# In each table's lookup VectorE waits once until its own second comparison has signalled

## The chip, the core and the metric

The kernel runs on one core of a Trainium2 chip. The metric is the device time of one execution in microseconds, lower is better. A core has TensorE (matmuls and transposes), VectorE, ScalarE, GpSimd and SyncE, each with its own in-order queue of instructions; they order their work among each other by semaphores. 16 DMA engines move data between HBM and the on-chip memories.

## The reference

512 samples each have 26 ids, one into each of 26 embedding tables of 128 columns, and a dense vector of 128. The dot products of all pairs among the 27 vectors are the features of a small network:

```python
e = jnp.stack([tbl_0[ids[:, 0]], ..., tbl_25[ids[:, 25]]], axis=1)
sd = jnp.einsum('bfd,bd->bf', e, dense)
ss = jnp.einsum('bfd,bgd->bfg', e, e)
z = jnp.concatenate([dense, sd, ss[:, iu, ju]], axis=1)
h = jnp.concatenate([z, dense], axis=1)
h = jnp.maximum(h @ W_top1 + b_top1, 0.0)
h = jnp.maximum(h @ W_top2 + b_top2, 0.0)
y = h @ W_top3
```

Everything is float32.

## The kernel before

Fourteen of the tables are read row by row with indirect DMAs by GpSimd (L269), 128 rows each time, and TensorE transposes what arrives (L507). The other twelve, the small ones of 1000 or 1250 rows, are read by matmul: the whole table is loaded into `table` (L221), 125 rows of the partition dimension by 8 or 10 chunks, and multiplied by a one-hot matrix of the ids. This work on one table is called a lookup here, and the tables are counted 0 to 11 in their order; table 3 has ten chunks, the others eight.

A lookup of table t has these steps:

- ScalarE copies the ids, relative to the table's rows, from PSUM to `ids_h` (`relate_ids`, L315).
- ScalarE rounds the table to a shorter float format: `high` (`split_high`, L325), one instruction for the table (two for table 0).
- VectorE makes `onehot`, one comparison for each chunk c (`make_onehot`, L378), 512 samples wide; each signals `onehot_ready`.
- VectorE subtracts `high` from `table` to get the remainder `low` (`split_low`, L386), in two halves of the chunks; each signals `low_ready`.
- TensorE multiplies `high` and `low` of each chunk with `onehot`, sixteen matmuls in one PSUM bank for a table of eight chunks (L472), and signals `table_selected`.
- ScalarE copies the bank into `embT` (L336), which signals `table_placed`.

The buffers `table`, `high`, `low` and `onehot` are threefold, so that the loading of table t + 3 waits for `low` of table t, and VectorE's work on table t + 3 waits for `table_selected` of table t.

VectorE's order is written out by hand in `step` (L390). While TensorE is at table t, VectorE has in its queue for table t + 1: comparisons 0 and 1, the first half of `low`, comparisons 2, 3 and 4 (2 to 5 with ten chunks), the second half of `low`, and the rest of the comparisons. Table 0 stands ahead of that loop (L426) with an order of its own. So the loop makes tables 1 to 11.

TensorE's order is the list `STEPS` (L185): T is a lookup, B a batch of transposes, D the dots of 128 samples (L527), C the copies of the dots into `pairs` (L309 on ScalarE, L371 on VectorE), L, M and Y the three layers. For the last two tables, 10 and 11, the lookup before D0 takes only the first 256 samples, and the other 256 come after D0 (L485). D0, the first dots, waits for all of `embT`'s first 128 samples (L511 to L517), thus also for ScalarE's copy of table 11's result. GpSimd's gathers are paced by `table_selected` (L264), and some later ones by `dots_done` (L266). After its last comparison VectorE adds two weight blocks (L405) and fills `pairs` (L407).

Of the kernel before, what the change touches and what calls it, by code (L numbers as in the profile page):

```python
# [49 lines left out]
def dlrm_tower(nc, gather_ids, onehot_ids, spread, tables, dense_t, w_pairs, w_dense, small, w2, identity,  # L50
# [19 lines left out]
    with ctx:  # L70
# [6 lines left out]
        def sem(name):  # L77
            return ctx.enter_context(nc.semaphore(name))
# [63 lines left out]
        onehot_ready = sem("onehot_ready")  # L142
# [19 lines left out]
        def half(i):  # L162
            return CHUNKS[i] // 2
# [4 lines left out]
        def onehots_to(i, chunk):  # L168
            return sum(CHUNKS[0:i]) + chunk + 1

        def highs_to(i, chunk):

            return sum(len(parts(n)) for n in range(i)) + sum(first <= chunk for first, _ in parts(i))
# [27 lines left out]
        def batch_no(t, b):  # L201
            return t * BATCHES + b

        def batch_placer(n):
            return PLACERS[n]
# [10 lines left out]
        @block.sync  # L216
        def _(sp):
            def load_rows(i, first, last, done):
                rows_of_part = tables[ONEHOT_TABLES[i]][:, :].rearrange("(p c) d -> p c d", c=CHUNKS[i])
                for a, b in ROW_PIECES:  # L220
                    sp.dma_start(table[i % TABLE_BUFFERS][a:b, first:last, :], rows_of_part[a:b, first:last, :]  # L221
                                 ).then_inc(done, 16)

            def load_table(i):
                if i >= TABLE_BUFFERS:
                    sp.wait_ge(low_ready, lows_to(i - TABLE_BUFFERS, CHUNKS[i - TABLE_BUFFERS] - 1))
                load_rows(i, 0, CHUNKS[i], table_loaded[i % TABLE_BUFFERS])

            def load_weights(n):
                dst, src = MLP_LOADS[n]  # L230
                sp.dma_start(dst, src).then_inc(mlp_loaded, 16)

            sp.dma_start(gather_idx[:, :, :], gather_ids).then_inc(gather_ids_loaded, 16)
            sp.dma_start(spread_f[0:ID_ROWS, :], spread).then_inc(spread_loaded, 16)
            for n, (first, last) in enumerate(parts(0)):
                load_rows(0, first, last, first_loaded[n])
            load_table(1)
            load_table(2)
            sp.dma_start(ident[:, :], identity).then_inc(ident_loaded, 16)
            load_table(3)  # L240
            load_table(4)
            sp.dma_start(denseT[:, :], dense_t).then_inc(dense_loaded, 16)
            load_table(5)
            for i in range(6, N_ONEHOT):
                load_table(i)
                if i - 6 < len(MLP_LOADS):
                    load_weights(i - 6)
            sp.wait_ge(y_ready, TILES)
            sp.dma_start(out, y).then_inc(stored, 16)
            sp.wait_ge(stored, 16)  # L250
# [27 lines left out]
        def place_batch(eng, copy, engine, t, b):  # L278
            eng.wait_ge(transposed, batch_no(t, b) + 1)
            n, s = BATCH_SIZE[b], FIRST_GATHERED_SLOT + BATCH_T * b  # L280
            copy(embT[:, t * TILE:(t + 1) * TILE, s:s + n].rearrange("p b s -> p s b"),
                 transposes_of(batch_no(t, b))[:, 0:n, :]).then_inc(batch_placed[engine], 1)
# [85 lines left out]
        @block.vector  # L368
        def _(dve):
            def copy(dst, src):  # L370
                return nc.vector.tensor_copy(dst, src)  # L371

            def make_onehot(i, first, last):
                if i >= STAGES:
                    dve.wait_ge(table_selected, i - STAGES + 1)
                dve.wait_ge(ids_relative, i + 1)
                for c in range(first, last):
                    nc.vector.tensor_scalar(onehot[i % STAGES][:, c, :], ids_h[:, i % ID_BUFFERS, :], float(c),  # L378
                                            None, ALU.is_equal).then_inc(onehot_ready, 1)

            def split_low(i, n):
                first, last = half(i) * n, half(i) * (n + 1)
                dve.wait_ge(high_ready, highs_to(i, first))
                if i >= STAGES:
                    dve.wait_ge(table_selected, i - STAGES + 1)
                nc.vector.tensor_tensor(low[i % STAGES][:, first:last, :], table[i % TABLE_BUFFERS][:, first:last, :],  # L386
                                        high[i % STAGES][:, first:last, :].bitcast(F32), ALU.subtract
                                        ).then_inc(low_ready, 1)

            def step(kind, t, i=0):  # L390
                if kind == "table" and i == 0:
                    if t + 1 < N_ONEHOT:
                        make_onehot(t + 1, 0, 2)
                        split_low(t + 1, 0)
                        make_onehot(t + 1, 2, half(t + 1) + 1)
                        split_low(t + 1, 1)
                        make_onehot(t + 1, half(t + 1) + 1, CHUNKS[t + 1])
                    if t == 2:
                        dve.wait_ge(dense_loaded, 16)
                        nc.vector.tensor_copy(embT[:, :, DENSE_SLOT].rearrange("p (a g u) -> p a u g", u=2, g=QUARTER),  # L400
                                              denseT[:, :].rearrange("p (a u g) -> p a u g", u=2, g=QUARTER)
                                              ).then_inc(dense_placed, 1)
                    if t + 1 == N_ONEHOT:
                        dve.wait_ge(mlp_loaded, MLP_LOADED)
                        nc.vector.tensor_tensor(wd[:, 0, :], wd[:, 0, :], wd[:, 1, :], ALU.add  # L405
                                                ).then_inc(weights_added, 1)
                        nc.vector.memset(pairs[0:32, :, :, :], 1.0).then_inc(pairs_filled, 1)  # L407
                elif kind == "batch" and batch_placer(batch_no(t, i)) == 1:
                    place_batch(dve, copy, 1, t, i)
                elif kind == "copies":  # L410
                    copy_dots(dve, copy, 1, t, i)
                elif kind == "relu2":
                    dve.wait_ge(layer2_done, CHUNKS2 * (t + 1))
                    nc.vector.tensor_scalar(h2[:, t % 2, 1, :], hidden[t % 2][:, 0, :], b2s[:, 1:2], 0.0,
                                            ALU.add, ALU.max).then_inc(h2_ready[1], 1)
                elif kind == "result":
                    dve.wait_ge(layer3_done, t + 1)
                    nc.vector.tensor_copy(y[:, t * TILE:(t + 1) * TILE], last_layers[0:1, TILE:2 * TILE]
                                          ).then_inc(y_ready, 1)

            nc.vector.memset(zeros[:, :], 0.0).then_inc(zeros_ready, 1)

            for first, last in ((ID_ROWS, 64), (64, 128)):
                nc.vector.memset(ids_f[first:last, :], 0.0).then_inc(ids_padded, 1)
            nc.vector.memset(embT[:, :, SLOTS:SLOT_PITCH], 0.0).then_inc(pads_zeroed, 1)
            for n in range(2):  # L426
                make_onehot(0, half(0) * n, half(0) * (n + 1))
                split_low(0, n)
            for s in STEPS:
                step(*s)  # L430
# [222 lines left out]
```

## Time and profile before

| | us |
|---|---|
| median of 3 runs | 114.46 (114.22 to 114.61) |
| profiled execution, its own time | 114.64 |
| span of the profiled execution | 112.8 |

The profile is one execution recorded by the hardware. Times within it are in us from the start of its span, durations in us too. PE is TensorE's matmuls, PEld its weight loads, DVE VectorE, ACT ScalarE, POOL GpSimd. In a timeline a row is: start, duration, engine, line, operation, output and inputs with their shapes, how many instructions are merged in the row, and in brackets how long the engine was idle before it and who released it. The start of a row and its duration give its recorded end. The recorded ends of TensorE are modelled, those of VectorE and ScalarE are not.

### The profile page before, as it was taken

Reading aid. Unit: us, or ns where it says so; the run is one execution under the profiler, and the core shown is the slowest. Engines: PE = TensorE matmul, PEld = TensorE weight load, DVE = VectorE, ACT = ScalarE, POOL = GpSimd, SP = SyncE. Lnnn points to the kernel's source line nnn. Section 1 sums busy time; section 2 is a strip of 40 time slices with the busy share of each in tenths; the row PEclk is TensorE's granted clock in tenths of the full one; section 3 lists DMA queues with packets and bytes.
Section 4 is the critical chain, followed back from the end, with each engine's and each line's share of the span. In section 5 each row is a group of like instructions: output and inputs, shape, how many; then the busy total and the mean of one; then the engine's idle time right before and its main releaser. Section 6 shows DMA issues by size and latency. Waiting matters only on the chain.

```text
span 112.8 us, 2831 instructions
## 1 busy us (share of the span) xinstructions
PE 104.5 (93%) x1095; PEld 91.8 (81%) x1095; DVE 84.2 (75%) x230; ACT 67.6 (60%) x153; POOL 60.8 (54%) x62
## 2 busy tenths in 40 slices
PE   6999999999999999499899979997999959996993
PEld 6866888888888887389799959997989949996890
DVE  4699999999999999999905891799169840885002
ACT  5545559789497387778425992768063950848120
POOL 7877777787777777776403775677257300000000
PEclk9999999999999999999999999999999999999999
DMA  2899999464999999611100122111202100000000
GB/s 72 233 269 200 242 249 265 94 210 105 325 264 328 302 259 312 155 51 47 47 9 0 47 54 71 29 47 47 52 12 58 47 6 6 0 0 0 0 6 1
DMA packets 5057, 12.75 MB, mean 113 GB/s; under 512 B 1690, under 2 KB 1818, under 8 KB 5044
## 3 DMA queue, kind: packets, MB, share of 16 engines
q1 hardware_dynamic: 3204, 8.83, 28.2%
q0 software_dynamic: 1792, 3.67, 12.3%
q8 instruction: 9, 0.15, 0.6%
q10 hardware_dynamic: 48, 0.07, 0.2%
q14 instruction: 4, 0.03, 0.1%
HBM read 12.56 MB, written 0.00 MB: 111 GB/s over the span
## 4 chain that ended last, share of the span: by engine, by line
PE 65%; ACT 10%; DVE 9%; DMA 7%; issue 4%; POOL 4%
PE dots L472 18%; PE dots L527 14%; PE hidden L552 12%; PE hidden L472 8%; ACT pairs L309 7%; DMA rows<-tbl,gather_idx 7%; DVE pairs L371 5%; POOL rows L269 4%; PE last_layers L451 3%; PE turned L507 2%; PE turned L552 2%; PE last_layers L576 2%; ACT h L350 2%; PE dots L445 2%; DVE onehot L378 1%
## 5 line engine op out<-in xcount | busy, mean ns | idle before, releaser
L269 POOL DMA_INDIRECT rows<-tbl,gather_idx x56 | 57.9, 1034 | 27.4 <-issue 14.8
L378 DVE TENSOR_SCALAR onehot<-ids_h 125x512 fp32r<-125x512 f16 x98 | 36.0, 426 | 0.9 <-ACT ids_h L315 0.9
L371 DVE COPY pairs<-dots 27x128 f32<-27x128 f32 (+8 forms) x88 | 23.7, 270 | 16.5 <-PE dots L527 13.8
L309 ACT COPY pairs<-dots 27x128 f32<-27x128 f32 (+8 forms) x88 | 21.0, 238 | 15.9 <-PE dots L527 13.8
L472 PE MATMUL dots<-onehot,high 125*128 125x512 f32 (+1 forms) x66 | 25.0, 399 | 0.0
L472 PE MATMUL dots<-onehot,low 125*128 125x512 f32 (+1 forms) x66 | 23.9, 381 | 0.1
L325 ACT CAST high<-table 125x1024 fp32r<-125x1024 f32 (+2 forms) x13 | 13.1, 1005 | 13.3 <-DMA table<-tbl 13.3
L527 PEld LDWEIGHTS dots<-embT 128*64 128x64 f32 x512 | 15.4, 138 | 2.8 <-issue 1.8
L527 PE MATMUL dots<-embT 128*64 128x54 f32 x512 | 15.8, 222 | 2.0 <-DVE embT L371 0.8
L386 DVE TENSOR_TENSOR low<-table,high 125x512 fp32r<-125x512 f32 (+1 forms) x24 | 16.6, 692 | 0.2 <-ACT high L325 0.2
L472 PEld LDWEIGHTS dots<-onehot,low 125*128 125x128 f32 x66 | 12.3, 188 | 2.8 <-DVE low L386 0.7
L472 PEld LDWEIGHTS dots<-onehot,high 125*128 125x128 f32 x66 | 12.4, 188 | 2.4 <-DVE onehot L378 0.2
L552 PE MATMUL hidden<-pairs,wp 128*128 128x128 f32 x112 | 13.4, 277 | 0.8 <-ACT pairs L309 0.8
L552 PEld LDWEIGHTS hidden<-pairs,wp 128*128 128x128 f32 x112 | 12.8, 192 | 1.3 <-ACT pairs L309 1.3
L472 PE MATMUL hidden<-onehot,high 125*128 125x512 f32 (+1 forms) x32 | 12.1, 389 | 0.0
L472 PE MATMUL hidden<-onehot,low 125*128 125x512 f32 (+1 forms) x32 | 11.4, 363 | 0.0
L336 ACT COPY embT<-dots 128x512 f32<-128x512 f32 (+1 forms) x8 | 8.5, 1065 | 0.4 <-PE dots L472 0.4
L315 ACT CAST ids_h<-dots 125x512 f16<-125x512 f32 x12 | 7.5, 624 | 1.3 <-PE dots L445 1.3
L309 ACT COPY embT<-turned 128x512 f32<-128x512 f32 x7 | 8.0, 1140 | 0.0
L507 PE MATMUL turned<-ident,rows 128*128 128x128 f32 x38 | 6.0, 276 | 1.6 <-DMA rows<-tbl,gather_idx 1.6
L472 PEld LDWEIGHTS hidden<-onehot,low 125*128 125x128 f32 x32 | 6.0, 189 | 0.9
L472 PEld LDWEIGHTS hidden<-onehot,high 125*128 125x128 f32 x32 | 6.0, 188 | 0.9
(55 smaller groups left out, 102.8 us busy)
## 6 DMA issues: line engine op xcount, KB each, us to landing
table<-tbl SPq DMA_DIRECT2D x10, 448.0 KB
wp<-w_pairs SPq DMA_DIRECT2D x2, 512.0 KB
rows<-tbl,gather_idx POOLq DMA_INDIRECT x56, 3.6
table<-tbl SPq DMA_DIRECT2D x1, 560.0 KB
table<-tbl SPq DMA_DIRECT2D x10, 52.0 KB
wd<-w_dense SPq DMA_DIRECT2D x1, 512.0 KB
w2s<-w SPq DMA_DIRECT2D x1, 512.0 KB
table<-tbl SPq DMA_DIRECT2D x2, 224.0 KB
```

The costliest lines, as they stand in the source:

```text
L269: pool.indirect_dma_start(out=rows[:, t % 2, n, :], out_offset=None, in_=tables[GATHERED_TABLES[n]][:, :], in_offset=bass.IndirectOffsetOn ...
L309: return nc.scalar.copy(dst, src)
L315: nc.scalar.copy(ids_h[:, i % ID_BUFFERS, :], relative[i % 2][0:ROW_PARTS, :]).then_inc(ids_relative, 1)
L325: nc.scalar.copy(high[i % STAGES][:, first:last, :], table[i % TABLE_BUFFERS][:, first:last, :]).then_inc(high_ready, 1)
L336: nc.scalar.copy(embT[:, samples, t], selected[t % STAGES][:, samples]).then_inc(table_placed, 1)
L371: return nc.vector.tensor_copy(dst, src)
L378: nc.vector.tensor_scalar(onehot[i % STAGES][:, c, :], ids_h[:, i % ID_BUFFERS, :], float(c), None, ALU.is_equal).then_inc(onehot_ready, 1)
L386: nc.vector.tensor_tensor(low[i % STAGES][:, first:last, :], table[i % TABLE_BUFFERS][:, first:last, :], high[i % STAGES][:, first:last, : ...
L472: last = nc.tensor.matmul(selected[t % STAGES][:, samples], part[t % STAGES][:, c, :], onehot[t % STAGES][:, c, samples], start=(part is h ...
L507: last = nc.tensor.transpose(transposes_of(n)[:, m, :], rows[:, t % 2, BATCH_T * i + m, :], ident[:, :])
L527: last = nc.tensor.matmul(dots[64 * h:64 * (h + 1), g, 0:2 * SLOTS], embT[:, s:s + 2, :].rearrange("p u s -> p (u s)"), embT[:, s:s + 2, 0 ...
L552: last = nc.tensor.matmul(hidden_block(t, m), wp[:, c, cols(m)], pairs[:, t % 2, c, :], start=False, stop=(c == PAIR_CHUNKS - 1), skip_gro ...
```

## The change

One wait is added in VectorE's queue, in each of the tables 1 to 11. `onehots_to(t + 1, 1)` is the count that `onehot_ready` has once comparison 1 of table t + 1 has signalled.

```diff
                 if kind == "table" and i == 0:
                     if t + 1 < N_ONEHOT:
                         make_onehot(t + 1, 0, 2)
+
+                        dve.wait_ge(onehot_ready, onehots_to(t + 1, 1))
                         split_low(t + 1, 0)
                         make_onehot(t + 1, 2, half(t + 1) + 1)
                         split_low(t + 1, 1)
```

`split_low(t + 1, 0)` reads `table` and `high` and writes `low`; it doesn't touch `onehot`.

## Rows read from the trace of the kernel before

**Rows 1.** The page: busy time and share of each engine; TensorE's granted clock in 40 slices.
```profile
PE 104.5 (93%) x1095; PEld 91.8 (81%) x1095; DVE 84.2 (75%) x230; ACT 67.6 (60%) x153; POOL 60.8 (54%) x62
...
PEclk9999999999999999999999999999999999999999
```

**Rows 2.** Busy time by stretches, 18 to 56 us, all engines, then granted clock.
```profile
18.00:56.00 38.00, 36.41 (x188) 30.38 (x186) 37.84 (x95) 28.30 (x35) 28.67 (x27) 1.00 0.68 197
```

**Rows 3.** The chain of waits: shares by engine, then pieces (start, duration, what).
```profile
PE 65%; ACT 10%; DVE 9%; DMA 7%; issue 4%; POOL 4%
...
39.17 7.75 DMA rows<-tbl,gather_idx
...
46.96 0.66 PE turned L507 x4
...
53.40 2.17 PE hidden L472 x16
...
55.59 0.60 ACT embT L336
...
56.33 3.96 PE dots L527 x128
```

**Rows 4.** Who waited for whom: us in total, times, longest.
```profile
DVE low L386 <- ACT high L325: 0.2, 1, 0.2
...
PEld dots L472 <- DVE onehot L378: 0.2, 1, 0.2
```

**Rows 5.** Timeline, the end of table 11, TensorE's weight loads and VectorE.
```profile
54.08 0.19 PEld L472 LDWEIGHTS hidden<-onehot,high 125*128 125x128 f32 x1
...
54.20 0.19 PEld L472 LDWEIGHTS hidden<-onehot,low 125*128 125x128 f32 x1
...
54.25 0.41 DVE L378 TENSOR_SCALAR onehot<-ids_h 125x512 fp32r<-125x512 f16 x1
...
54.58 0.41 DVE L378 TENSOR_SCALAR onehot<-ids_h 125x512 fp32r<-125x512 f16 x1
...
54.72 0.19 PEld L472 LDWEIGHTS hidden<-onehot,high 125*128 125x128 f32 x1
...
55.05 0.19 PEld L472 LDWEIGHTS hidden<-onehot,high 125*128 125x128 f32 x1
```

**Rows 6.** Timeline, table 1: ScalarE's `high`, VectorE from its second comparison on.
```profile
9.31 1.05 ACT L325 CAST high<-table 125x1024 fp32r<-125x1024 f32 x1 [0.81 <-DMA table<-tbl]
...
9.75 0.41 DVE L378 TENSOR_SCALAR onehot<-ids_h 125x512 fp32r<-125x512 f16 x1
...
10.40 0.69 DVE L386 TENSOR_TENSOR low<-table,high 125x512 fp32r<-125x512 f32 x1 [0.24 <-ACT high L325]
11.01 0.42 DVE L378 TENSOR_SCALAR onehot<-ids_h 125x512 fp32r<-125x512 f16 x1
```

**Rows 7.** Timeline of VectorE, first `low` of tables 6 and 7 with its neighbours.
```profile
31.82 0.68 DVE L386 TENSOR_TENSOR low<-table,high 125x512 fp32r<-125x512 f32 x1
...
35.42 0.42 DVE L378 TENSOR_SCALAR onehot<-ids_h 125x512 fp32r<-125x512 f16 x1
35.76 0.68 DVE L386 TENSOR_TENSOR low<-table,high 125x512 fp32r<-125x512 f32 x1
36.36 0.41 DVE L378 TENSOR_SCALAR onehot<-ids_h 125x512 fp32r<-125x512 f16 x1
```

**Rows 8.** Timeline of VectorE after the lookups.
```profile
55.76 0.91 DVE L407 MEMSET pairs<- 32x1024 f32 x1 [0.15 <-issue]
...
60.31 6.59 DVE L371 COPY pairs<-dots 27x128 f32<-27x128 f32 x22 [3.64 <-PE dots L527]
```

**Rows 9.** Timeline, table 4: second half of `low`, and the weight load that needs it.
```profile
25.55 0.67 DVE L386 TENSOR_TENSOR low<-table,high 125x512 fp32r<-125x512 f32 x1
...
26.39 0.19 PEld L472 LDWEIGHTS dots<-onehot,low 125*128 125x128 f32 x1
```

**Rows 10.** Timeline, table 11: ScalarE's `high` and VectorE's first `low`.
```profile
48.54 1.05 ACT L325 CAST high<-table 125x1024 fp32r<-125x1024 f32 x1 [1.15 <-DMA table<-tbl]
...
51.52 0.74 DVE L386 TENSOR_TENSOR low<-table,high 125x512 fp32r<-125x512 f32 x1
```

## The prediction

> **What bounds the kernel now.** I read the page's engine shares first [rows 1]. TensorE is busy for 93% of the span, VectorE for 75%, and the granted clock is at its upper level, 2.4 GHz, from the second slice on. A change on VectorE then seems harmless, and the share is the wrong place to stop: VectorE's 75% is an average over a lookup stage in which it never rests and a later stage in which it often does. The table by stretches shows it: from 18 to 56 us VectorE is busy for 37.84 of 38.00 us, TensorE for 36.41 [rows 2]. So the question becomes which of the two ends the lookups.
>
> The chain of waits [rows 3] says TensorE, at first sight. It goes through a gather that lands at 46.92, the transposes at 46.96, and TensorE's last four runs of lookups, to 55.57. From there ScalarE's copy of the last table's result into `embT` (L336) takes 0.60 us, and the first dots (L527) start at 56.33. Everything after that is queued behind these dots.
>
> But the chain goes back through whatever engine worked without a long gap, and small gaps hide in it. The list of waits has TensorE's weight loads waiting once for a comparison, 0.2 us [rows 4]. The timeline of the last table [rows 5] shows where. TensorE loads the weights for c = 4 of `high` at 54.08 and of `low` at 54.20, a step of 0.12 us. VectorE's last two comparisons (c = 6 and 7) begin at 54.25 and 54.58 and take 0.41 us each, to 54.66 and 54.99. The weight loads of `high` that need them start at 54.72 and 55.05, each 0.06 us behind. Had TensorE kept its step, the last would have been five steps after 54.20, at 54.80 rather than 55.05. So in the last table TensorE walks at VectorE's pace, and VectorE's queue is the later one by 0.25 us. Two chains run side by side, and the one printed is not the one that ended last.
>
> VectorE's queue is unbroken before that: in the tables after the first it waited for another engine once [rows 4], 0.24 us at 10.40, for ScalarE's `high` of table 1 [rows 6]. A table of eight chunks costs it 3.94 us, from a `low` at 31.82 to the same one at 35.76 [rows 7].
>
> **What the change adds.** Nothing is removed or moved, no instruction that computes is added, and no DMA. In each of the tables 1 to 11 VectorE now waits, between its second comparison and the first `low` subtraction (L386), until that second comparison has signalled. The subtraction doesn't read the comparison's result; the wait only orders them. Queued behind it on VectorE are the subtraction, the other six comparisons, the second subtraction, and all later tables. Those who wait for these are TensorE, SyncE's load of the table three later (by `low_ready`), and ScalarE's `relate_ids`.
>
> The trace of before has no wait of VectorE for itself, so its price comes from two rows. First the overlap that is lost. The second comparison of table 7 starts at 35.42 and takes 0.42 us, to 35.84. The subtraction starts at 35.76 [rows 7], 0.08 us before the recorded end. A wait for its signal can't be over before that end. Then the hand-over from signal to start. ScalarE's `high` of table 1 starts at 9.31 and takes 1.05 us, to 10.36; the waiting subtraction starts at 10.40 [rows 6], which is 0.04 us. It is the same instruction on the same engine behind a real wait, so I take it: 0.08 + 0.04 = 0.12 us for each wait. Does the subtraction itself become faster when it starts alone? The one at 10.40 takes 0.69 us and the next comparison starts 0.61 us after it [rows 6]; the one at 35.76 takes 0.68 us and the next starts 0.60 us after it [rows 7]. No, so nothing is given back.
>
> Bounds for one wait: the lower one is the overlap alone, 0.07 us when the rounding of two rows is allowed for. A gain is excluded, since the order of the work is the same and no engine gets anything earlier. The upper one is 0.08 + 0.15 = 0.23 us, with the longest gap that VectorE shows between two of its own instructions without a named releaser, 0.15 us at 55.76 before the memset of `pairs` [rows 8].
>
> The hidden part: table 1's wait is covered. Its second comparison starts at 9.75 and ends near 10.16, and the subtraction waits for `high` until 10.40 anyway [rows 6]. Ten waits are left: 10 x 0.12 = 1.2 us, from 10 x 0.07 = 0.7 to 10 x 0.23 = 2.3.
>
> Does the 1.2 us reach the end? VectorE's last comparison ends at 54.99 + 1.2 = 56.2, and TensorE's last matmul, `embT`'s copy and the first dots follow at the same distance, the dots at about 57.5. What was TensorE's own chain is no longer near. It is late once on the way: in table 4 the weights of `low` for c = 4 load at 26.39, and the subtraction that makes them starts at 25.55 and takes 0.67 us, to 26.22 [rows 9]. That leaves 0.17 us, against three counted waits by then (tables 2, 3, 4), 0.36 us. TensorE loses some 0.2 us there, and the gathers that are paced by its `table_selected` lose as much. Its chain then ends near 55.57 - 0.25 + 0.2 = 55.5, well before the 55.57 + 1.2 = 56.8 of VectorE's. So no second bill is added. Other users of the delay have room: ScalarE's last `high` is cast at 48.54 to 49.59 and first read at 51.52 [rows 10], 1.9 us.
>
> After the first dots I find no slack to soak it up: DMA has 7% of the whole chain, and the one gather before 46.96, 7.75 us of 112.8, is all of it [rows 3]. From 56.33 on the chain is TensorE, VectorE and ScalarE in turn. The memset of `pairs`, done at 56.67 [rows 8], moves to 57.9, and its readers are VectorE's copies, which start at 60.31 now [rows 8] and 61.5 then.
>
> The sum against the profiled execution's own time, 114.64 us (span 112.8 and 1.8 around it): 115.8. That execution is 0.18 us above the median of 114.46, so against the median it is 114.46 + 1.2 = 115.7 us, 1.0% slower.
>
> A page of the Trainium skill speaks against any cost. "VectorE: DVE Perf Modes", section "The DRAIN you can't avoid", states that the next operation doesn't start until the pipe is empty and that a semaphore after each operation cost nothing in eight copies. The rows do not fit its first half: the subtraction starts 0.08 us before the comparison's recorded end [rows 7]. By that page the sum would be zero; it is the first rival below.
>
> **Rivals.**
> 1. Not slower. If the signal of a comparison is out at the moment when the next instruction may start anyway, the wait is already over when the subtraction's turn comes, the recorded end being only a late record. Place: each of the ten waits; price 0.00 to 0.02 us; time 114.3 to 114.6. It decides if the overlap of 0.08 us is a matter of records alone. For it: VectorE's rows overlap by the same 0.08 us everywhere. Against it: TensorE's weight loads, which need those comparisons, start 0.06 us after the recorded end and never before it [rows 5], and `high` to `low` shows 0.04 us after the end [rows 6]. Chance 0.09.
> 2. A dearer hand-over. Waiting for itself, VectorE may have to take up the next instruction afresh once the signal is there, where now it has it ready. Then 0.15 to 0.23 us for each, 1.5 to 2.3 in sum, 116.0 to 116.8 us. For it: the 0.15 us gap at 55.76 [rows 8]. Against it: 0.04 us at 10.40 [rows 6]. Chance 0.20.
> 3. Partly covered. TensorE's chain or the gathers end the lookups, or some waits fall where VectorE has time. Then 0.4 to 0.8 us, 114.9 to 115.2. For it: the chain of waits names TensorE and a gather [rows 3]. Against it: the weight loads that trail the comparisons by 0.06 us [rows 5]. Chance 0.08.
> 4. The forecast, 0.09 to 0.14 us for each of ten, 115.3 to 115.9: chance 0.60.
> The rest, 0.03, is a faster kernel by a cause that I don't see.
>
> **Numbers.** The likeliest is 115.7. The range goes from 115.1 (0.07 us each, nearly all of case 3 left out) to 116.7 (0.22 us each), which leaves out cases 1 and some of 2 and 3. A measurement of this kernel can tell about 0.3%, 0.34 us, from no change. Slower by more: cases 2, 3 and 4, 0.88. Within: 0.09. Faster: 0.03.
>
> **What would show it.** In the profile after, every first `low` of tables 2 to 11 has a gap of about 0.04 us before it instead of an overlap of 0.08 us, and the distance from one to the next grows from 3.94 to 4.06 us. The last comparison ends near 56.2, and the last table's weight loads of `high` again trail the comparisons by 0.06 us, now from c = 5 on, after a wait for the second subtraction. The first dots start near 57.5, and from there to the end the distance is as before. The prediction is wrong if the distance stays at 3.94 us (case 1), if it is 4.1 or more (case 2), or if it grows and the first dots don't move as much (case 3).

## The result and the profile after

| | us |
|---|---|
| median of 4 runs, changed kernel | 116.35 (115.72 to 119.19) |
| median of the kernel before, same comparison | 114.38 (114.22 to 114.61) |
| ratio | 1.0152, interval 1.0082 to 1.0223 |
| profiled execution, its own time | 115.72 |
| span of the profiled execution | 113.9 |

The changed kernel is slower, by 0.8 to 2.2% by the interval. The four executions were 115.72, 115.86, 116.84 and 119.19 us; the last, 3% above the fastest and with a granted clock of 0.985 of the upper level on average, is left out of the ratio. The median of 116.35 takes it in, that of the three others is 115.86. The profiled pair differs by 115.72 - 114.64 = 1.08 us.

VectorE's timeline around the first `low` of table 7 in the changed kernel, which answers to [rows 7]:

```profile
36.05 0.41 DVE L378 TENSOR_SCALAR onehot<-ids_h 125x512 fp32r<-125x512 f16 x1
36.50 0.69 DVE L386 TENSOR_TENSOR low<-table,high 125x512 fp32r<-125x512 f32 x1
37.11 0.42 DVE L378 TENSOR_SCALAR onehot<-ids_h 125x512 fp32r<-125x512 f16 x1
...
40.56 0.69 DVE L386 TENSOR_TENSOR low<-table,high 125x512 fp32r<-125x512 f32 x1
```

The second comparison ends at 36.46 and the subtraction starts at 36.50, after a gap of 0.04 us, where it overlapped the comparison by 0.08 us before. The subtraction is as long as it was, and the next comparison starts 0.61 us after it. From one first `low` to the next it is 4.06 us; it was 3.94.

The end of table 11 and the first dots, all engines' timeline, which answers to [rows 3, 5]:

```profile
54.38 0.68 DVE L386 TENSOR_TENSOR low<-table,high 125x512 fp32r<-125x512 f32 x1
54.98 1.09 DVE L378 TENSOR_SCALAR onehot<-ids_h 125x512 fp32r<-125x512 f16 x3
...
55.11 0.19 PEld L474 LDWEIGHTS hidden<-onehot,low 125*128 125x128 f32 x1 [0.35 <-DVE low L386]
...
55.45 0.19 PEld L474 LDWEIGHTS hidden<-onehot,high 125*128 125x128 f32 x1 [0.15 <-DVE onehot L378]
...
56.12 0.18 PEld L474 LDWEIGHTS hidden<-onehot,high 125*128 125x128 f32 x1
...
56.66 0.59 ACT L336 COPY embT<-hidden 128x256 f32<-128x256 f32 x1 [2.56 <-PE hidden L474]
...
57.39 0.33 PE L529 MATMUL dots<-embT 128*64 128x54 f32 x4 [0.33 <-ACT embT L336]
```

VectorE's last comparison ends at 54.98 + 1.09 = 56.07, 1.08 us later than before, and the last weight load of `high` trails it by 0.05 us. The first dots start at 57.39, 1.06 us later. From there to the end of the span it is 113.9 - 57.4 = 56.5 us, as it was (112.8 - 56.3). All of the loss lies ahead of the first dots.

In the chain of waits VectorE has now 19% of the span, where it had 9% [rows 3]. The page's line:

```profile
PE 59%; DVE 19%; ACT 10%; DMA 5%; issue 4%; SPq 0%; DVEq 0%
```

### The profile page after: what moved, and what is told of

It reads as the page before. It is cut to its first block, busy times and chain, and to the rows that moved or that the text cites. A ratio compares the mean times of both kernels' runs of the same rounds, so it can differ in the third digit from the quotient of the medians.

```text
span 113.9 us, 2833 instructions
## 1 busy us (share of the span) xinstructions
PE 106.4 (93%) x1095; PEld 92.4 (81%) x1095; DVE 84.9 (75%) x230; ACT 67.3 (59%) x153; POOL 60.8 (53%) x62
## 4 chain that ended last, share of the span: by engine, by line
PE 59%; DVE 19%; ACT 10%; DMA 5%; issue 4%; SPq 0%; DVEq 0%
PE dots L529 14%; PE dots L474 14%; PE hidden L554 11%; DVE onehot L378 10%; PE hidden L474 8%; ACT pairs L309 7%; DVE pairs L371 5%; DMA table<-tbl 5%; DVE low L386 3%; PE last_layers L453 3%; PE turned L554 2%; PE last_layers L578 2%; ACT h L350 2%; PE dots L447 2%; PE turned L509 2%
## 5 line engine op out<-in xcount | busy, mean ns | idle before, releaser
L453 PE MATMUL last_layers<-zeros 128*128 128x128 f16 x47 | 5.1, 289 | 1.0 <-DVE zeros L423 1.0
```

The source lines that it names most:

```text
L453: nc.tensor.matmul(last_layers[:, 0:128], zeros[:, :], zeros[:, :], start=True, stop=True)
```

## The experiments

The first result left three things open. Is the price that of the drained comparison or that of the wait itself? Does it grow with the number of waits? Is VectorE's queue really what comes last? Twelve runs were made on four other chips, and each has a trace of one execution. On three of these four chips all kernels, before's too, took 128 us or more throughout, with TensorE's granted clock at 0.88 to 0.97 on average, so their end times can't be set beside 114.46; VectorE's stretches of instructions can, since most of them keep their lengths; where they don't, the text says so.

| run | this kernel, median (lowest to highest, n) | before on the same chip |
|---|---|---|
| e1 wait on the second | 132.97 (130.67 to 134.22, 12) | 147.48 (131.36 to 153.57, 18) |
| e2 wait on the first | 148.62 (147.09 to 152.87, 6) | as e1 |
| e3 two waits | 133.77 (131.72 to 134.31, 6) | as e1 |
| e4 wait standing alone | 134.44 (131.44 to 136.64, 6) | as e1 |
| e5 wait on the second | 115.62 (115.45 to 116.74, 6) | 131.02 (114.09 to 131.65, 11) |
| e6 wait on the first | 123.37 (114.58 to 131.48, 6) | as e5 |
| e7 copy late | 131.49 (128.47 to 140.67, 6) | 149.49 (129.62 to 152.34, 11) |
| e8 copy late, wait | 130.32 (128.87 to 132.24, 6) | as e7 |
| e9 copy late, even tables | 130.48 (128.73 to 138.20, 6) | as e7 |
| e10 two waits | 132.78 (128.90 to 133.36, 6) | as e7 |
| e11 light | 131.90 (131.25 to 134.62, 5) | 150.22 (132.04 to 153.94, 9) |
| e12 light, wait | 132.88 (130.86 to 135.61, 5) | as e11 |

**e1 and e5: the changed kernel again.** No edit.

> The changed kernel once more, in more rounds, to have its size and its scatter. Theory (each wait costs the lost overlap of 0.08 us and a hand-over of 0.03 to 0.04 us, ten waits count, and VectorE's queue ends the lookups): 1.1 us over the kernel before, ratio 1.010, and a profile in which each first low of tables 2 to 11 starts 0.03 us after the comparison's recorded end. Rival (something beyond the ten waits also costs, as the scatter of the first result from 115.72 to 116.84 may say): 1.6 us or more, ratio 1.014 or more, with dots that start later than 57.5 us or a longer way from them to the end.

> The changed kernel again; on the chip of the first four runs TensorE's granted clock fell and the gathers stood still for long in both kernels, so that the end times there say little. Theory: 1.1 us over the kernel before, ratio 1.010, low 0.034 us after the comparison's recorded end. Rival (more than the ten waits costs): ratio 1.014 or more.

e5 is the clean measurement of size: ratio 1.0136, interval 1.0080 to 1.0193, five of the six executions between 115.45 and 115.82 beside 114.09 to 114.39 for the five executions of before that were not near 131. The medians of these two fives are 115.47 and 114.29, 1.18 us apart, and the lowest are 1.36 us apart. Its first dots start at 57.16. The sixth took 116.74 us; what makes two of the nine counted executions of this kernel 1 us longer stays open, and it is why the ratio's middle lies above 1.010. The rival of 1.014 or more is thus neither shown nor out by the ratio. The traces of both runs have the gap of the theory in nearly every table, and the distance from one first `low` to the next is 4.06 or 4.07 us in most of them.

e1's ratio, 0.9962 (0.9862 to 1.0062), can't be read for this question. But its medians hold something that no theory here had foreseen: 132.97 against 147.48. That is taken up behind the next runs.

**e2 and e6: the wait on the first comparison.**

```diff
-                        dve.wait_ge(onehot_ready, onehots_to(t + 1, 1))
+                        dve.wait_ge(onehot_ready, onehots_to(t + 1, 0))
```

> The same wait in the same place, but on the signal of the first comparison, which is 0.33 us older. Theory (what costs is the end of the second comparison, not the wait instruction): same as the kernel before, within 0.1 us, low again 0.08 us before the recorded end. Rival (the extra wait instruction or the taking up of the next one costs by itself): 0.5 to 1.1 us slower.

> The wait on the first comparison's signal again. Its trace had low 0.08 us ahead of the comparison's recorded end as before, 3.94 us for a table. Theory: within 0.3% of the kernel before. Rival (the extra wait instructions cost by themselves): 0.5 us or more slower.

VectorE's timeline in e2, table 7, the second comparison with its first, and the first `low`s of tables 7 and 8:

```profile
34.81 0.74 DVE L378 TENSOR_SCALAR onehot<-ids_h 125x512 fp32r<-125x512 f16 x2
35.47 0.68 DVE L386 TENSOR_TENSOR low<-table,high 125x512 fp32r<-125x512 f32 x1
...
39.41 0.68 DVE L386 TENSOR_TENSOR low<-table,high 125x512 fp32r<-125x512 f32 x1
```

The comparison ends at 35.55 and the subtraction starts at 35.47: the overlap of 0.08 us is back, and a table takes 3.94 us, with the wait instruction still there. So the instruction costs nothing in VectorE's queue; having to see the comparison's end costs 0.12 us. The end times of e2 and e6 follow those of the kernel before, not those of the changed kernel, in a way that the expectation had not named: 147 to 153 us in e2, and between 114.58 and 131.48 in e6. So the forecast of "within 0.3%" for e6 rests on one execution, 114.58 us. Two others, 116.64 and 116.70 us, are 2 us above it without being near 131, and no trace of such an execution was kept.

**e4: the same wait, standing alone.** The program gives an instruction one wait of its own; other waits stand ahead as instructions. In the changed kernel the wait for the comparison is the one that `low` carries. Here it is put last in the source, and the trace has it in an instruction of its own in front of `low`, together with the wait for `table_selected`, while `low` carries the wait for `high`.

```diff
-            def split_low(i, n):
+            def split_low(i, n, own=False):
...
+                if own:
+                    dve.wait_ge(onehot_ready, onehots_to(i, 1))
                 nc.vector.tensor_tensor(low[i % STAGES][:, first:last, :], ...
...
-                        split_low(t + 1, 0)
+                        split_low(t + 1, 0, own=True)
```

> The same wait on the second comparison, but put last among the waits of the first low, so that it is a wait instruction of its own in front of low, and low itself carries the wait for high. Theory (the hand-over of 0.03 us goes by low being parked with the wait that comes last): if low has to be taken up afresh after the wait instruction, its start comes 0.05 to 0.15 us later, and the kernel is 1.6 to 2.6 us over the kernel before. Rival (the form of the wait doesn't matter): 1.1 us over it, as with the changed kernel.

VectorE's timeline in e4, table 7:

```profile
36.09 0.41 DVE L378 TENSOR_SCALAR onehot<-ids_h 125x512 fp32r<-125x512 f16 x1
36.64 0.69 DVE L388 TENSOR_TENSOR low<-table,high 125x512 fp32r<-125x512 f32 x1
```

From 36.50 to 36.64 are 0.14 us, where the carried wait leaves 0.04. The first `low` before it is at 32.48, 4.16 us away, and other tables of this trace take 4.16 to 4.22 us. The form of the wait matters: the price of one wait is 0.22 us or a little more standing alone, 0.12 us carried. This is the rival of the prediction with the dearer hand-over, and it is real, but in another form of the program. The end time can't be compared for the reason above.

**e3 and e10: two waits in each table.**

```diff
                         make_onehot(t + 1, 2, half(t + 1) + 1)
+                        dve.wait_ge(onehot_ready, onehots_to(t + 1, half(t + 1)))
                         split_low(t + 1, 1)
```

> The changed kernel with a second such wait in each table, ahead of the second half of low, on the comparison just before it. Theory: each wait has the same price wherever it stands, so eleven more of 0.11 us, 1.2 us more than with one, 2.3 us over the kernel before. Rival (VectorE runs into slack elsewhere, or TensorE and the gathers take over as the bound): clearly less than 2 us, and a rival on the other side (late VectorE makes TensorE and the gathers late too) 2.7 us or more.

> Two waits in each table again. The trace of the first try had 0.034 us gaps before both halves of low and 4.19 us for a table. Theory: 21 or 22 waits of 0.12 us, 2.4 us over the kernel before, ratio 1.021. Rival (TensorE's or the gathers' chain takes over or is dragged along): under 1.9 or over 2.9 us. No gather instruction held for over 2 us.

VectorE's timeline in e3, tables 6 and 7:

```profile
34.36 0.69 DVE L386 TENSOR_TENSOR low<-table,high 125x512 fp32r<-125x512 f32 x1
...
35.64 0.42 DVE L378 TENSOR_SCALAR onehot<-ids_h 125x512 fp32r<-125x512 f16 x1
36.09 0.69 DVE L386 TENSOR_TENSOR low<-table,high 125x512 fp32r<-125x512 f32 x1
...
38.55 0.69 DVE L386 TENSOR_TENSOR low<-table,high 125x512 fp32r<-125x512 f32 x1
```

In this table the second wait costs what the first does: 35.64 + 0.42 = 36.06 to 36.09 is a gap of 0.03 us, and the table takes 38.55 - 34.36 = 4.19 us, 3.94 + 2 x 0.12 = 4.18. In others it costs more: four tables of e3 and five of e10 took 4.3 to 4.4 us. VectorE's timeline in e10, table 10:

```profile
50.35 0.69 DVE L386 TENSOR_TENSOR low<-table,high 125x512 fp32r<-125x512 f32 x1
...
52.14 0.74 DVE L386 TENSOR_TENSOR low<-table,high 125x512 fp32r<-125x512 f32 x1
52.80 1.94 DVE L378 TENSOR_SCALAR onehot<-ids_h 125x512 fp32r<-125x512 f16 x5
54.78 0.74 DVE L386 TENSOR_TENSOR low<-table,high 125x512 fp32r<-125x512 f32 x1
```

The table takes 54.78 - 50.35 = 4.43 us. Its gaps are 0.04 us as elsewhere, but the second subtraction takes 0.74 us instead of 0.68, and five comparisons take 1.94 us instead of 1.81. From table 1's first `low` to table 11's it is 54.78 - 10.20 = 44.58 us in e10, 3.46 us more than the 41.12 us of the kernel before, and 44.34 us in e3. That is 0.16 to 0.17 us for each of the twenty waits between them, not 0.12. So the expectation of 2.3 or 2.4 us was missed in VectorE's queue, on the side that e10 had named as its rival, over 2.9 us; why the instructions themselves grew longer stays open. The sum in the end time isn't shown, since neither run fell on a chip where it could be read.

**e7, e8 and e9: taking work out of VectorE's way.** The copy of the dense features moves behind the last comparison, without the wait (e7), with it (e8), with it in the even tables only (e9).

```diff
-                    if t == 2:
+                    if t + 1 == N_ONEHOT:
                         dve.wait_ge(dense_loaded, 16)
                         nc.vector.tensor_copy(embT[:, :, DENSE_SLOT].rearrange(...
```

> The kernel before with VectorE's copy of the dense features (0.56 us of its queue, at 22.60 in the trace of before) moved behind the last comparison, no wait added. Theory (VectorE's queue ends the lookups, by 0.25 us ahead of TensorE's own chain): 0.25 us faster than the kernel before, about 0.2%. Rival (TensorE and the gathers end them): no difference. In executions in which a gather's instruction on GpSimd is held by VectorE's unbroken queue (13.9 and 23.05 us in two traces of the wait on the first comparison), the move should make no difference: some executions near 131 us remain, as in the kernel before.

> The changed kernel with the same copy moved. Theory: VectorE's queue is 1.12 us longer by the waits and 0.56 us shorter by the move, so 0.56 us over the kernel before, 0.5 us under the changed kernel. Rival (the end of the lookups isn't VectorE's): same as the changed kernel. No gather instruction held for over 2 us, since VectorE has a gap in each table.

> As the one before, but the wait only in tables 2, 4, 6, 8 and 10. Theory for the length: five waits of 0.112 us, 0.56 us, against a move of 0.56 us, so level with the kernel before to 0.1 us. Theory for the gathers (a gap of 0.034 us in VectorE's queue lets a held gather instruction through): a hold can last two tables, 8 us, at most, and most executions stay near 114.5 us; if it needs more than that, executions of 117 us and more remain.

VectorE's last comparison ends at 54.64 in e7, 0.35 us earlier than in the trace of before and not 0.56, although table 1's first `low` starts 0.30 us earlier: six tables took 4.06 us with no gap in them. Timelines of VectorE, table 6, e7 and then e8:

```profile
31.09 0.68 DVE L386 TENSOR_TENSOR low<-table,high 125x512 fp32r<-125x512 f32 x1
31.69 1.21 DVE L378 TENSOR_SCALAR onehot<-ids_h 125x512 fp32r<-125x512 f16 x3
...
35.15 0.68 DVE L386 TENSOR_TENSOR low<-table,high 125x512 fp32r<-125x512 f32 x1
```

```profile
31.91 1.09 DVE L378 TENSOR_SCALAR onehot<-ids_h 125x512 fp32r<-125x512 f16 x3
```

Without the wait the three comparisons behind the first `low` take 1.21 us here, with it 1.09, and the table takes 4.06 us in both. From table 1's first `low` to table 11's it is 41.18 us in e7 without a wait, 41.20 in e9 with five and 41.70 in e8 with ten. So on this chip ten waits made VectorE's queue 0.5 us longer and not 1.2, and its last comparison ends 0.37 us later (55.01 in e8). The gap is there each time, but the comparisons can give back as much; what makes them longer in e7 stays open. It is one trace of each kernel. The end times don't settle the theory either: in e7's trace ScalarE's copy behind the last table came late (the first dots start at 58.90 though the last weight load of a lookup is at 54.80). Inconclusive for the end of the lookups, and the hoped-for version that beats both kernels is not shown. In e9's trace the tables with a wait are longer than those without, in the same queue:

```profile
31.32 0.69 DVE L386 TENSOR_TENSOR low<-table,high 125x512 fp32r<-125x512 f32 x1
...
35.28 0.68 DVE L386 TENSOR_TENSOR low<-table,high 125x512 fp32r<-125x512 f32 x1
...
39.33 0.69 DVE L386 TENSOR_TENSOR low<-table,high 125x512 fp32r<-125x512 f32 x1
```

3.96 us to table 7's, which has no wait ahead of it, and 4.05 us to table 8's, which has one.

**e11 and e12: VectorE made light.** Comparisons 2 and 3 of tables 3 to 11 work on 64 of the 512 samples, so most of these one-hot columns are not written anew. The two kernels leave out 7/8 of these comparisons.

```diff
+                    width = 64 if i >= STAGES and c in (2, 3) else BATCH
-                    nc.vector.tensor_scalar(onehot[i % STAGES][:, c, :], ids_h[:, i % ID_BUFFERS, :], float(c),
+                    nc.vector.tensor_scalar(onehot[i % STAGES][:, c, 0:width], ids_h[:, i % ID_BUFFERS, 0:width], ...
```

> The kernel before with comparisons 2 and 3 of tables 3 to 11 only 64 samples wide instead of 512, which leaves out 7/8 of these comparisons (the rest of their one-hot columns keeps what was there). That takes some 0.23 us from each of 18 comparisons, 4 us of VectorE's queue, so that TensorE alone ends the lookups. Theory: VectorE now stands idle for TensorE in each table, the lookups end 0.25 us earlier than in the kernel before, and, because VectorE's queue has gaps, no gather instruction on GpSimd is held for over 2 us, without any added wait. Rival for the holds (it is the added wait itself and not a gap that lets GpSimd through): holds of 10 us and more as in the kernel before.

> The same with the added wait. Theory (the wait costs time only where VectorE's queue is what comes last): no difference to the run without the wait, within 0.1 us, although the eleven waits are there with their 0.112 us each in VectorE's queue. Rival (the waits delay TensorE or the gathers on their way too): 0.3 us or more slower than without.

Timelines, VectorE's last comparisons and TensorE's last weight load of a lookup, e11 and then e12:

```profile
52.30 0.74 DVE L379 TENSOR_SCALAR onehot<-ids_h 125x512 fp32r<-125x512 f16 x2
...
56.81 0.19 PEld L473 LDWEIGHTS hidden<-onehot,low 125*128 125x128 f32 x1
```

```profile
52.74 0.74 DVE L379 TENSOR_SCALAR onehot<-ids_h 125x512 fp32r<-125x512 f16 x2
...
56.31 0.19 PEld L475 LDWEIGHTS hidden<-onehot,low 125*128 125x128 f32 x1
```

Without the wait VectorE is done at 53.04, with it at 53.48, and TensorE's lookups end 3.8 and 2.8 us later, at 56.81 and at 56.31. VectorE's delay of 0.44 us didn't reach them. That agrees with the theory of the path, that the wait is free where VectorE has a lead of some us, but doesn't prove it: the two traces differ by 0.5 us the other way, where 0.1 us was expected, and the medians, 131.90 and 132.88 us, are nearer to each other than the executions of either kernel. The expectation of e11 that VectorE stands idle in each table was wrong: it ran without a gap till 44, and waited twice behind that.

**What held the gathers.** Why does the kernel before reach 131 us on a chip where it also makes 114.09, while the changed kernel stays at 115.45 to 116.74? The trace of e6, an execution of that kind, shows it. GpSimd, VectorE and TensorE:

```profile
24.16 23.05 POOL L269 DMA_INDIRECT rows<-tbl,gather_idx  x1 [0.30 <-PE dots L474]
...
45.29 1.10 DVE L378 TENSOR_SCALAR onehot<-ids_h 125x512 fp32r<-125x512 f16 x3
...
47.52 0.94 POOL L269 DMA_INDIRECT rows<-tbl,gather_idx  x1 [0.30 <-issue]
...
52.46 0.48 PE L509 MATMUL turned<-ident,rows 128*128 128x128 f32 x1 [15.87 <-DMA rows<-tbl,gather_idx]
```

One gather instruction on GpSimd, 0.94 us in the median of this trace, lasts 23.05 us, from 24.16 to 47.21. In these 22 us VectorE is never idle, as busy time by stretches says (e6, all engines: length, then TensorE's matmuls, its weight loads, VectorE, ScalarE, GpSimd, then the granted clock):

```profile
24.16:46.39 22.23, 12.43 (x59) 9.98 (x57) 22.23 (x58) 14.10 (x17) 22.23 (x1) 0.83 0.77 217
...
52.46:56.00 3.54, 3.54 (x11) 2.99 (x12) 0.00 (x0) 1.49 (x2) 2.83 (x3) 0.50 0.24 60
```

VectorE's last comparison ahead of a stop ends at 46.39, and the gather instruction ends 0.82 us later. TensorE waits 15.87 us for the rows; it had come to a stand at 52.46 - 15.87 = 36.59. Behind that stand its granted clock is 0.50, the lower level, 1.2 GHz, from 52.46 to 56.00. VectorE's stop at 46.39 is a wait for TensorE: its next comparison starts at 58.74, after 12.35 us. e2 has the same at another place:

```profile
41.88 13.91 POOL L269 DMA_INDIRECT rows<-tbl,gather_idx  x1 [1.90 <-remote]
...
54.29 0.68 DVE L407 TENSOR_TENSOR wd<-wd 128x512 f32<-128x512 f32 x1
```

The instruction ends at 55.79, again 0.82 us after VectorE's queue came to a gap, at 54.97. While GpSimd is held, VectorE's tables are a little shorter: 35.30 - 31.41 = 3.89 us in e6 against 3.94:

```profile
31.41 0.70 DVE L386 TENSOR_TENSOR low<-table,high 125x512 fp32r<-125x512 f32 x1
...
35.30 0.70 DVE L386 TENSOR_TENSOR low<-table,high 125x512 fp32r<-125x512 f32 x1
```

In the seven traces of full kernels with a drained comparison in each table (the changed kernel, e1, e3, e4, e5, e8, e10), and in that of e9, no gather instruction lasts more than 1.67 us. But each is a trace of one execution, and the trace of before has no hold either; no long execution of the kernel before itself was traced. The times say more: the 42 executions of e1, e3, e4, e5, e8 and e10 lie, kernel by kernel, within 5.2 us of each other; those of the kernel before lie 17 to 23 us apart on each of the four chips, and 33 of its 49 are 8 us or more above the chip's lowest. e9, with the wait in five tables, has one execution of six, 138.20 us, that is 9.5 us above its lowest, which the expectation had allowed for if a hold lasts two tables at most; it wasn't traced. The Trainium skill, "SBUF — State Buffer", section "Who interferes with whom", has a rule that bears on it: VectorE's two-port modes and GpSimd exclude each other from a shared pair of ports, and a paragraph in its section "SBUF: two separate sides" says that the descriptors of GpSimd's DMAs can then not be written. By that page the hold would last one VectorE instruction; the trace has 58 in the stretch, and no run shows in which mode they ran. So the ports are a guess at the mechanism. What the runs show is that a gap of 0.03 us in each table went together with no long hold.

What is not shown is that the gap alone does it. e7 has no added wait and no hold in its trace, though two of its six executions, not traced, were at 138.93 and 140.67. e11 has an unbroken queue till 44 us and none of its five executions was above 134.62, beside seven of nine of before above 147. So an unbroken queue makes a hold possible and doesn't always make one. What starts it stays open. A kernel with a gap made in another way wasn't tried.

## Why the prediction was right, and where it was not

**The path.** Right. VectorE's queue ended the lookups, hidden behind a chain of waits that named TensorE. Its last comparison moved by 1.08 us and the first dots by 1.06. e11 and e12 agree with the other side, that the wait is free with a lead of some us, without proving it.

**The price of one wait.** Right: 0.08 us of lost overlap and 0.04 us of hand-over, 0.12 in sum, measured as 4.06 - 3.94. e2 shows that it is the drain and not the instruction. The prediction took the rest of the queue to be fixed, and that is not so everywhere: on the chip of e7 and e8 the comparisons gave back more than half of ten waits, and with two waits in each table other instructions grew longer. The first `low` of table 1 was covered by `high`, as said: it started at 10.43 instead of 10.40.

**The sum.** From table 1's first `low` to table 11's it was 51.52 - 10.40 = 41.12 us and is 52.76 - 10.43 = 42.33: 1.21 us for ten waits, as predicted. Of these 0.16 us came back in table 11: from its first `low` to the end of the last comparison it was 54.99 - 51.52 = 3.47 us and is 56.07 - 52.76 = 3.31. Three comparisons that took 1.21 us there in the trace of before take 1.09 now. Table 1 started 0.03 us later. So it is 1.21 - 0.16 + 0.03 = 1.08 us in the profiled pair where 1.2 were forecast.

**The number.** The executions taken together say more than the profiled pair: 1.5% and a median of 116.35 us, where 1.0% and 115.7 us were the likeliest. One of its three counted executions took 116.84 us, and the median also takes in the one of 119.19. Neither was traced, and nothing in the prediction's sum stands for them. So the size of the wait is borne out by the profiled pair and by e5 (1.18 us between medians), and that the median still lies within 115.1 to 116.7 us is in part luck: the upper part of the range was meant for a dearer hand-over, which didn't come.

**TensorE on its way.** The mechanism was right and the place and size were off. In table 4 it waits for the first half of `low`, not the second:

```profile
24.25 0.69 DVE L386 TENSOR_TENSOR low<-table,high 125x512 fp32r<-125x512 f32 x1
...
24.99 0.19 PEld L474 LDWEIGHTS dots<-onehot,low 125*128 125x128 f32 x1 [0.42 <-DVE low L386]
...
26.72 0.19 PEld L474 LDWEIGHTS dots<-onehot,low 125*128 125x128 f32 x1
```

The load of [rows 9] moves from 26.39 to 26.72, by 0.33 us, not 0.2. The gathers were to become as much later, and did not: TensorE's wait of 1.6 us for rows ahead of table 9 is gone, and the transposes ahead of it start at 45.56 instead of 46.96. Why these rows came earlier in a kernel with a longer queue stays open. TensorE also waits 0.22 us for table 3's first half, at 19.49, and in table 11 for both halves of `low`. Neither changes the end.

**The rivals.** "Not slower" fell for lack of its condition: the signal is not out before the recorded end, else the gap of 0.04 us would be none. The prediction took only half of what the Trainium skill says on the drain: "VectorE: DVE Perf Modes", section "The DRAIN you can't avoid", adds that a next operation that isn't held starts earlier. The traces agree with that: where nothing makes it wait, it starts 0.08 us before the recorded end, in e2 too. The eight copies of that section compare semaphores that are signalled; here a signal that is waited for costs 0.12 us. The dearer hand-over didn't come in the changed kernel; in e4, where the wait stands alone, it took 0.14 us.

**The step that failed.** "A gain is excluded, since the order of the work is the same and no engine gets anything earlier." In the changed kernel's own trace TensorE has the rows ahead of table 9 by 45.56 instead of 46.92, and on other chips GpSimd, it seems, gets through where VectorE's unbroken queue held it. The prediction looked for those who wait for VectorE by a semaphore and not for those whom it holds up without one. Nothing in the trace of before shows a hold; its gathers take 0.94 to 1.48 us each. On the chip of the first result no execution of before shows it in its time, all four lie between 114.22 and 114.61 us, and the changed kernel is 1.5% slower. On the two chips where the changed kernel was run again its median is some 15 us below that of the kernel before (115.62 against 131.02, 132.97 against 147.48), and the missing holds are the only difference found that could account for it. The forecast time holds for most executions without a hold and says nothing on the others.

## What to carry to other kernels

A wait of an engine on its own last instruction costs the overlap of the two and the hand-over, here 0.12 us, and 0.22 us if the wait stands as an instruction of its own. How much of it reaches the queue's length can differ, from 0.05 us each (e8 beside e7) to 0.17 (e10). It counts only where that engine's queue comes last, which small repeated waits of 0.06 us at the consumer tell better than the chain of waits does. Before such a wait is called a pure loss, look at what a queue without any gap keeps others from: compare the longest instruction of GpSimd with the median one, over many executions and on more than one chip. One median of three executions, as in the table at the head, can miss a second way in which the same program runs.

## What the runs showed of the hardware

- Two VectorE instructions without a wait between them overlap by 0.08 us by the record (before, e2); a signal that has to be seen moves the next start to 0.03 or 0.04 us after the recorded end if the instruction carries the wait, and to 0.14 us if the wait stands ahead of it (e4).
- A gather instruction on GpSimd took 13.91 us (e2) and 23.05 us (e6) beside a VectorE queue without a gap, where most take 0.94 to 1.5 us, and ended 0.82 us after the queue's first stop in both traces.
- TensorE's granted clock was 0.50 when it took up work again after a stand of 15.87 us (e6).
- With GpSimd held, VectorE's table takes 3.89 us, with GpSimd at work 3.94, and in e7's trace 4.06 in six tables, where three comparisons take 1.21 us instead of 1.09.
- With two waits in each table (e10) some subtractions take 0.74 us instead of 0.68, and the ten tables from 1 to 10 take 3.46 us more than before, where twenty gaps alone would make 2.4.
